# Last stage of a convolution, attention and expert kernel: loop written out, another order on TensorE and VectorE, GpSimd adds eight experts to four

## What is computed

```
t = t + attention(layernorm(t))                        # and attention's own residual
z = layernorm(t)
p = softmax(z @ router_w + router_b)                   # 8 experts
top_p, top_i = top_k(p, 2);  top_p = top_p / sum(top_p)
t = t + sum over the two of top_p * (z @ expert_w[top_i] + expert_b[top_i])
out = t, back as (16, 32, 56, 56)
```

## Time and profile before

| | us |
|---|---|
| median of three runs | 2783.09 |
| profiled execution, its own time | 2785.88 |
| its span in the trace | 2784.1 |
| VectorE busy | 2365.9 (85%) |
| TensorE busy (matmuls) | 2433.0 (87%) |
| ScalarE busy | 1600.0 (57%) |
| GpSimd busy | 406.9 (15%) |
| mean granted TensorE clock | 0.908 |

### The profile page before, as it was taken

One profiled execution on the slowest core, in us unless ns is written; L12 is line 12 of the kernel. 1 busy time (PEld: TensorE's weight loads), 2 busy tenths in 40 slices (PEclk: granted clock), 3 DMA queues, 4 the chain that ended last, 5 costly groups with the idle time before them and its releaser, 6 DMA issues. The chain is left out here.

```text
span 2784.1 us, 48279 instructions
## 1 busy us (share of the span) xinstructions
PE 2433.0 (87%) x18454; PEld 985.0 (35%) x18454; DVE 2365.9 (85%) x4218; ACT 1600.0 (57%) x2106; POOL 406.9 (15%) x456
## 2 busy tenths in 40 slices
PE   3888878379999999999999999999999987777776
PEld 1343333112222222222222222222222246666665
DVE  4567776689999999999999999999999927888886
ACT  1143343247777777777777777777777753233232
POOL 0021121300000000000000000000000004445455
PEclk9989999579999999999999999999999986666666
DMA  7687692510210221201202202202200011223221
GB/s 172 172 222 225 188 271 96 169 33 1 59 40 21 59 94 30 59 22 38 59 10 50 59 1 59 59 1 59 59 1 24 24 53 65 71 74 101 70 70 24
DMA packets 68108, 206.19 MB, mean 74 GB/s; under 512 B 20630, under 2 KB 33554, under 8 KB 61234
## 3 DMA queue, kind: packets, MB, share of 16 engines
q1 hardware_dynamic: 64034, 185.27, 24.0%
q0 software_dynamic: 3040, 15.57, 1.5%
q10 hardware_dynamic: 816, 2.46, 0.3%
HBM read 80.14 MB, written 61.31 MB: 51 GB/s over the span
## 5 line engine op out<-in xcount | busy, mean ns | idle before, releaser
L1333 DVE TENSOR_REDUCE at_XM<-at_psX 128x1 f32<-128x448 f32 x2688 | 1546.2, 619 | 92.2 <-PE at_psX L1184 71.3
L1250 ACT ACTIVATE at_PR<-at_psS 128x896 f32<-128x896 f32 x1344 | 1162.9, 915 | 455.0 <-PE at_psS L1160 452.9
L1202 PE MATMUL at_psV<-at_PR,at_V 128*32 128x448 f32 x5376 | 645.2, 552 | 0.1
L1160 PE MATMUL at_psS<-at_US,at_KS 128*128 128x448 f16 x2688 | 636.2, 356 | 1.7 <-DMA at_US<-at_mrow 1.1
L1184 PE MATMUL at_psX<-at_KS,at_US 64*128 64x448 f16 x1344 | 490.4, 365 | 65.2 <-DVE at_XM L1333 42.8
L1184 PE MATMUL at_psX<-at_KS,at_UH 64*128 64x448 f16 x1344 | 490.4, 365 | 0.0
L1184 PEld LDWEIGHTS at_psX<-at_KS,at_US 64*128 64x128 f16 x1344 | 124.6, 93 | 721.2 <-DVE at_XM L1333 661.5
L1160 PEld LDWEIGHTS at_psS<-at_US,at_KS 128*128 128x128 f16 x2688 | 200.9, 98 | 274.3 <-ACT at_PR L1250 119.3
L1299 POOL CAST at_mrow<-at_mt 7x128 f16<-7x128 f32 x64 | 17.9, 279 | 1613.3 <-DVE at_mt L1352 1260.4
L1602 POOL TENSOR_TENSOR fi_WE<-fi_WE 128x256 f32<-128x256 f32 (+1 forms) x224 | 212.9, 979 | 172.8 <-DVE fi_WE L1656 172.1
L1656 DVE TENSOR_TENSOR fi_WE<-fi_psE,fi_WT 128x512 f32<-128x512 f32 (+1 forms) x208 | 132.7, 666 | 43.9 <-PE fi_psE L1505 33.9
(11 more groups left out here) (205 smaller groups left out, 2101.4 us busy)
## 6 DMA issues: line engine op xcount, KB each, us to landing
sums<-at_O SPq DMA_DIRECT2D x16, 1568.0 KB, 6.3
fi_SUMS<-sums SPq DMA_DIRECT2D x16, 1568.0 KB, 6.6
sb_stacks<-sb_T SPq DMA_DIRECT2D x64, 270.5 KB, 7.2
sb_stacks<-sb_Xp SPq DMA_DIRECT2D x64, 248.8 KB, 8.4
sb_stacks<-sb_Xp SPq DMA_DIRECT2D x64, 248.0 KB, 5.6
sb_stacks<-sb_T SPq DMA_DIRECT2D x64, 172.5 KB, 10.0
at_KS<-key_stacks SPq DMA_DIRECT2D x32, 208.0 KB, 6.8
fi_RES<-residual SPq DMA_DIRECT2D x16, 400.0 KB, 7.0
```

The source lines that it names most:

```text
L1160: last = nc.tensor.matmul(psS[:, at % 2, k, 0:TILE], KS[:, b, (2 * c + k) * P:(2 * c + k + 1) * P], US[:, b, t * TILE:(t + 1) * TILE], sta ...
L1202: last = nc.tensor.matmul(psV[C * q:C * q + C, 0:TILE], V[:, b, G * k + q, :], PR[:, (n * 2 * STEPS + 2 * q4 + q // 2) % PRS, q % 2, :], s ...
L1250: nc.scalar.activation(PR[:, f % PRS], psS[:, at % 2, :, 0:TILE], ACT.Exp).then_inc(p_ready, 1)
L1333: nc.vector.tensor_reduce(o, psX[:, (at + j) % 3, 0:TILE], AX.X, ALU.max).then_inc(x_done, 1)
```

## The change

1. finish is written out for all steps, without the loop; beyond and the register waits go.
2. TensorE's order in a step becomes: project(n + 1) both halves; experts(n - 1, 2 to 6); then six times four or five token transposes and one of the units 7 to 12; the router's first set after unit 10 and the others after unit 12; experts(n, 0 1); sums(n - 1).
3. VectorE's order becomes: weigh 0 and 1 ahead of the sum over channels, weigh 2 ahead of centring, weigh 3 4, sum of squares, weigh 5, root, scale, weigh 6, Z16, weigh 7 to 12, invert both halves and divide the first, top-k, divide the second. The mean is no longer an instruction of its own.
4. The end of the top-k chain multiplies by the reciprocal once instead of twice.
5. newton_rsqrt has three instructions instead of four, in prepare too.
6. GpSimd adds only eight to four, 7 additions an image. TensorE sums the four and T1: five matmuls a set, 70 records an image.

```
 def newton_rsqrt(link, eng, r, v, t):
     link(eng.tensor_tensor(t, r, r, ALU.mult))
-    link(eng.tensor_tensor(t, t, v, ALU.mult))
-    link(eng.tensor_scalar(t, t, -0.5, 1.5, ALU.mult, ALU.add))
-    return link(eng.tensor_tensor(r, r, t, ALU.mult))
+    link(eng.scalar_tensor_tensor(out=t, in0=t, scalar=-0.5, in1=v, op0=ALU.mult, op1=ALU.mult))
+    return link(eng.scalar_tensor_tensor(out=r, in0=t, scalar=1.5, in1=r, op0=ALU.add, op1=ALU.mult))
...
-        def steps(eng, step):
-            for n in range(FIRST):
-                step(n, n % TURN, n // 2)
-            with eng.Fori(0, (N - TURN) // TURN) as i:
-                for n in range(FIRST, FIRST + TURN):
-                    step(i * TURN + n, n % TURN, i * 2 + n // 2)
-            for n in range(N - 1, N + 1):
-                step(n, n % TURN, n // 2)
+        def steps(step):
+            for n in range(N + 1):
+                step(n, n % TURN, n // 2)
...
-                    for e in range(E // 4 + 1):
-                        v = (WE[:, s, e] if e < E // 4 else T1[:, c, G * s:G * s + w // C]).rearrange("p q c -> p (q c)")
+                    for e in range(E // 2 + 1):
+                        v = (WE[:, s, e] if e < E // 2 else T1[:, c, G * s:G * s + w // C]).rearrange("p q c -> p (q c)")
...
                 if more:
-                    project(n + 1, mb, r + b, (0,))
-                if old:
-                    experts(m, mb, (2, 3, 4))
-                if more:
-                    project(n + 1, mb, r + b, (1,))
-                if old:
-                    experts(m, mb, (5, 6))
+                    project(n + 1, mb, r + b)
+                if old:
+                    experts(m, mb, range(2, 7))
                 if new:
                     pe.wait_ge(z16_ready, n + 1)
                     pe.wait_ge(z_high, n * 2 + 2)
-                for s in range(KSETS):
+                for i, u in enumerate(range(7, NU)):
                     if new:
-                        turn_tokens(n, s)
+                        turn_tokens(n, range(NC * i // (NU - 7), NC * (i + 1) // (NU - 7)))
                     if old:
-                        experts(m, mb, (s + 7,))
+                        experts(m, mb, (u,))
+                    if new and u == 10:
+                        router(n, b, 0)
                 if new:
-                    router(n, b)
-                if old:
-                    experts(m, mb, (11, 12))
-                if new:
+                    for k in range(1, KSETS):
+                        router(n, b, k)
                     experts(n, b, (0, 1))
                 if old:
                     sums(m, mc)
...
-                if beyond(n, 0):
-                    for s in range(QSETS + 1):
-                        if s < QSETS:
-                            pool.wait_ge(we_ready, n * NU - NU + min(2 * s + 2, NU))
-                            fold(s, E // 2).then_inc(half_folded, 1)
-                        if s >= 1:
-                            pool.wait_ge(half_folded, n * QSETS - QSETS + s)
-                            fold(s - 1, E // 4).then_inc(folded, 1)
+                if n > 0:
+                    for s in range(QSETS):
+                        pool.wait_ge(we_ready, n * NU - NU + min(2 * s + 2, NU))
+                        fold(s, E // 2).then_inc(folded, 1)
...
-                weigh(m, mb, (0,))
+                weigh(m, mb, (0, 1))
                 dve.wait_ge(t1_ready, n + 1)
                 mark(nc.vector.tensor_reduce(lsum[:], T1[:, c], AX.X, ALU.add))
+                weigh(m, mb, (2,))
                 settled()
-                mark(nc.vector.tensor_scalar(lsum[:], lsum[:], 1.0 / C, None, ALU.mult))
-                weigh(m, mb, (1,))
-                settled()
-                nc.vector.tensor_tensor(XH[:], T1[:, c], per_token(lsum[:]), ALU.subtract).then_inc(t1_cen, 1)
-                weigh(m, mb, (2,))
+                nc.vector.scalar_tensor_tensor(out=XH[:], in0=per_token(lsum[:]), scalar=-1.0 / C, in1=T1[:, c],
+                                               op0=ALU.mult, op1=ALU.add).then_inc(t1_cen, 1)
+                weigh(m, mb, (3, 4))
                 dve.wait_ge(t1_sq, n + 1)
                 link(nc.vector.tensor_reduce(lvar[:], SQ[:], AX.X, ALU.add))
                 nc.vector.tensor_scalar(lvar[:], lvar[:], 1.0 / C, LN_EPS, ALU.mult, ALU.add).then_inc(t1_var, 1)
-                weigh(m, mb, (3, 4))
+                weigh(m, mb, (5,))
...
                 nc.vector.memset(XH[:, :, 0:1], 1.0).then_inc(xh_ready, 1)
+                weigh(m, mb, (6,))
...
-                weigh(m, mb, range(5, NU))
+                weigh(m, mb, range(7, NU))
+                if nxt:
+                    invert(n + 1, 0)
+                    invert(n + 1, 1)
+                    settled()
+                    divide(n + 1, (c + 1) % TURN, 0)
...
+                dve.wait_ge(gap_exp, n + 1)
+                mark(nc.vector.tensor_scalar(g1[:], g2[:], 1.0, None, ALU.add))
                 settled()
+                mark(nc.vector.tensor_tensor(SEL2[:], SEL2[:], per_token(g2[:], E), ALU.mult))
+                mark(nc.vector.reciprocal(g1[:], g1[:]))
                 settled()
+                link(nc.vector.tensor_tensor(SEL1[:], SEL1[:], SEL2[:], ALU.add))
+                mark(nc.vector.tensor_tensor(WT[:, b], SEL1[:], per_token(g1[:], E), ALU.mult))
                 if nxt:
                     divide(n + 1, (c + 1) % TURN, 1)
-                dve.wait_ge(gap_exp, n + 1)
-                link(nc.vector.tensor_scalar(g1[:], g2[:], 1.0, None, ALU.add))
-                link(nc.vector.reciprocal(g1[:], g1[:]))
-                mark(nc.vector.tensor_tensor(g2[:], g2[:], g1[:], ALU.mult))
-                mark(nc.vector.tensor_tensor(SEL1[:], SEL1[:], per_token(g1[:], E), ALU.mult))
                 settled()
-                link(nc.vector.tensor_tensor(SEL2[:], SEL2[:], per_token(g2[:], E), ALU.mult))
-                link(nc.vector.tensor_tensor(WT[:, b], SEL1[:], SEL2[:], ALU.add))
```

More of the change, by code:

```diff
@@ L42 @@
 GR = 2 * XW
-ORDER_0, ORDER = 15, 51
-ORDER_F = 29
+ORDER_0, ORDER = 14, 46
 class Ahead(NamedTuple):
@@ L1456, in step @@
                 b = c % 2
-                if beyond(n, 0) and (not isinstance(n, int) or n + 1 < N):
+                if n > 0 and n + 1 < N:
                     load(n + 1, 1 - b)
-                if beyond(n, 1):
+                if n > 1:
                     store(n - 2, b)
-            steps(sp, step)
+            steps(step)
             store(N - 1, 1)
@@ L1468, in _, with project @@
         def _(pe):
[L1469 to L1473, removed]
-                    if beyond(n, 0):
+            def project(n, b, r):
+                pe.wait_ge(sums_in[b], (r + 1) * 16)
+                for h in range(2):
+                    if n > 0:
                         pe.wait_ge(o_done, n * 2 + h - 1)
@@ L1526, in step @@
                 m, mb, mc = n - 1, 1 - b, (c - 1) % TURN
-                old = beyond(n, 0)
-                new = not isinstance(n, int) or n < N
-                more = not isinstance(n, int) or n + 1 < N
+                old = n > 0
+                new = n < N
+                more = n + 1 < N
                 if more:
-                    project(n + 1, mb, r + b, (0,))
+                    project(n + 1, mb, r + b)
                 if old:
-                    experts(m, mb, (2, 3, 4))
-                if more:
-                    project(n + 1, mb, r + b, (1,))
-                if old:
-                    experts(m, mb, (5, 6))
+                    experts(m, mb, range(2, 7))
                 if new:
@@ L1555, in _ @@
             pe.wait_ge(fin.w_ready, 1)
-            project(0, 0, 0, (0, 1))
-            steps(pe, step)
+            project(0, 0, 0)
+            steps(step)
         @block.scalar
@@ L1570, in step @@
                 b = c % 2
-                if not isinstance(n, int) or n < N:
+                if n < N:
                     act.wait_ge(t1_cen, n + 1)
@@ L1587, in step @@
                         act.wait_ge(k_full, n * KSETS + s + 1)
-                        if s == 0 and beyond(n, 1):
+                        if s == 0 and n > 1:
                             act.wait_ge(e_full, n * NU - NU)
@@ L1594, in step @@
                     nc.scalar.activation(g2[:], gap[:], ACT.Exp).then_inc(gap_exp, 1)
-            steps(act, step)
+            steps(step)
             to_image(N - 1, 1, (N - 1) // 2)
@@ L1629, in _ @@
             done = [0]
-            base = [0]
             def mark(ins):
@@ L1636, in settled @@
             def settled():
-                dve.wait_ge(order, base[0] + done[0])
+                dve.wait_ge(order, done[0])
             def link(ins):
@@ L1652, in weigh @@
                     dve.wait_ge(e_full, n * NU + u + 1)
-                    if u % 2 == 0 and beyond(n, 0):
+                    if u % 2 == 0 and n > 0:
                         dve.wait_ge(set_done, n * QSETS - QSETS + u // 2 + 1)
@@ L1675, in step @@
```

(7 more changed lines are left out.)

81 lines of the change are left out of this document (36 added, 45 removed).

## The result

| | kernel before | changed kernel |
|---|---|---|
| median, us | 2782.77 (2777.23 to 2784.76, 4 runs) | 2801.78 (2799.86 to 2804.66, 4 runs) |
| profiled execution, its span | 2785.88, 2784.1 | 2803.19, 2801.3 |

The ratio is 1.0064 (95% interval 1.0052 to 1.0076): the change costs 19 us. The forecast was 2844, slower by 61. Its sign is right, its size is not. Two executions lie far off all others and are in none of the ratios, one of 2871.66 us of the kernel before and one of 5190.82 us of the kernel before with its loop written out; nothing here shows what made them slow.

The account below looks back on a forecast made before the run. The prediction took VectorE's instruction order to bound the kernel before. Last-stage images +67.3, image 0 -2.7, the end -1.5 and first stage -2 made +61 on 2785.9, 2847; that execution being 2.8 above the median, 2844 (range 2797 to 2880).

Parts of the forecast that it names:

- The step held to be decisive: On TensorE, 50 projection records ahead of experts 2 to 6 take 8.1 us; weighing 2 starts 8.4 late.
- weighing 2 to the first token: VectorE's stretch from weighing 2 to the next image's first token transposition, forecast to go from 8.9 to 9.9 us.
- first token to the sums: TensorE from first token transposition to start of sums, forecast 7.1 us for 7.6, bounds 6.3 and 8.1.
- sums, 70 records: TensorE's sums with 28 more records at 0.118 each, forecast 9.4 us for 6.1, bounds 8.3 to 10.4.
- projection and hand-over: TensorE between sums and weighing 2: projection 8.1 us, expert 2's two matmuls and the hand-over 0.7.
- top-k of 6.4: VectorE's top-k, forecast to fall from 10.1 to 6.4 us through lost stretches, line 1741, inversions and first division.
- the end: After 2764, GpSimd's 12.18 us falls to about 8.5, TensorE partly replacing it: -1.5 us (0 to -4.5).
- rival (1): TensorE's clock holds: sums 8.3, projection 6.0, image 32.0 us, in all 2803 us; chance 0.20.
- The first stage: 20 Newton chains each lose one instruction of 0.2 us, DMA waits hiding about half: -2 us (0 to -4.4).
- The new wait for the residual: VectorE's sum over channels waits for GpSimd's 1.88 us residual, until 2.1 us after weighing 0.
- TensorE's seven sets take its place in part: After 2764, TensorE's seven sets replace only part of GpSimd's saved time, within the forecast of -1.5 us.
- Rival (3): TensorE does not hold VectorE in the last stage: 26.8 us an image, 2732 us in all; chance 0.07.

Follow-up runs that it names:

- the best kernel: Changed kernel with one projection half moved behind expert 3 and the other behind expert 6: 2728.05 us, 0.9793 of the kernel before.
- the experiment on the clock: Changed kernel with one wait added, TensorE starting each step's sums only when VectorE has the top-k chain's gap: 2886.09 us, a single execution.

## Why the prediction was right in its mechanism, and which step of it failed

**The step held to be decisive is the cause.** Both halves of the projection ahead of expert 2 hold weighing 2. Put into the kernel before alone, this costs 15.6 us; put back as it was in the changed kernel, it gives back 15.6, most of the 19. The 74 us of the best kernel are another comparison: a place that neither kernel had, behind expert 3 and behind expert 6, which also frees what the other parts had won and the old place hides.

**The pieces of an image**, images 2 to 14, forecast against measured:

| piece | forecast | measured, mean (range) |
|---|---|---|
| weighing 2 to the first token | 9.9 | 9.97 (9.97 to 9.98) |
| first token to the sums | 7.1 | 6.46 (6.02 to 6.88) |
| sums, 70 records | 9.4 | 8.00 |
| projection and hand-over | 8.8 | 7.62 (6.02 to 8.56) |
| image | 35.2 | 32.06 |

VectorE's piece is exact, and its top-k of 6.4 too (2328.82 to 2335.22 in image 1). All three pieces of TensorE came out short, together 3.2 us an image. With VectorE's 0.07 against it the image is 3.14 short, 40.9 over 13, and the median missed by 42. That the rest is so small is partly luck, since larger misses beside it cancel: the end took 4.8 more than forecast, and the last stage began 5.8 earlier in this execution. The largest term is the sums. I took 70 records at a clock that rises during them, since that is how 11 of the 14 were before. All 14 of the changed kernel ran at the high clock; windows of line 1510 alone (columns us, PE, PEld, clock, DMA), the first two and the sum of the 14:

```profile
2328.71:2336.71 8.00, 8.00 (x70) 7.68 (x70) 1.00 0.01 2
2361.84:2369.84 8.00, 8.00 (x70) 7.69 (x70) 1.00 0.01 2
...
sum 112.00, PE 111.98 PEld 107.55; mean PE 8.00 PEld 7.68
```

Before, TensorE paused twice between the last tokens and the sums, 1.2 to 1.8 us in all (the expectation of the experiment on the clock has 1.0 to 1.3, which is too little). The clock had risen ahead of the sums in 11 of the 14 steps; in 8 of these it fell again around their start, in 3 it held, and in the other 3 steps it rose only during the sums. But the length of the pause alone does not decide: with the same two pauses, 0.32 and 1.01, the clock held in one step and fell in another. TensorE's timeline behind the second pause and a window over the sums, once for each:

```profile
2364.59 0.61 PE L1505 MATMUL fi_psE<-fi_wz,fi_ZS 128*128 128x256 f16 x4 [1.01 <-DVE fi_WE L1656]
2365.10:2369.90 4.80, 4.80 (x43) 4.51 (x42) 4.56 (x11) 0.23 (x1) 2.92 (x5) 1.00 0.00 0
...
2545.84 0.61 PE L1505 MATMUL fi_psE<-fi_wz,fi_ZS 128*128 128x256 f16 x4 [1.01 <-DVE fi_WE L1656]
2546.80:2550.10 3.30, 3.30 (x17) 3.30 (x17) 3.09 (x8) 0.00 (x0) 2.47 (x5) 0.50 0.00 0
```

With experts 7 to 12 among the tokens and the router split, one pause of 0.6 to 0.8 is left, the clock rose ahead of all 14 sums and held, and so it did in all kernels here with that order but the one with the pause added. That the order is what does it fits all of them; which part of it, the shorter pause or the denser work ahead, is not shown. The start came 0.6 earlier on average, the more so the sooner the clock rose: 6.02 us from the first token to the sums where it rose 3.0 us after the first token, 6.88 where it rose after 5.1. Sums and start together are 2.0 of the 3.2.

The second term is the projection. I let the clock fall 2.6 to 3.9 us after the sums, in the middle of the projection; it fell after 3.0 to 6.0 in these 13 images. Windows of line 1465 alone, three images:

```profile
2466.71:2474.80 8.09, 8.09 (x50) 7.95 (x50) 0.69 0.01 3
2500.11:2507.53 7.42, 7.42 (x50) 7.28 (x50) 0.76 0.00 0
2532.01:2537.77 5.76, 5.76 (x50) 5.65 (x50) 1.00 0.01 3
```

The first is the 8.1 of my sum, the last is rival (1)'s 6.0, and the mean lies between. The fall itself, in the second of them:

```profile
2501.10:2504.00 2.90, 2.90 (x28) 2.90 (x27) 0.58 (x1) 0.00 (x0) 0.78 (x1) 0.99 0.00 0
2504.00:2505.00 1.00, 1.00 (x7) 1.00 (x6) 0.00 (x0) 0.00 (x0) 0.00 (x0) 0.50 0.00 0
```

TensorE is busy without a gap on both sides of it (by the modelled ends of the trace), as before. By the Trainium skill, "TensorE: Matmul & The Clock Gate", section on why this matters for your kernels, TensorE kept busy holds the high clock; for the sums that is what happened, for the projection it is not.

So **rival (1)**, at 32.0 an image and 2803, came nearest in time, but its mechanism holds for the sums only, and in 10 of 13 images not for the whole projection. That it meets the time is luck: its projection of 6.0 is too short, and its start of 7.1 and sums of 8.3 too long by about as much. The failed step is the price of the sums and of the projection, both taken at the old kernel's clock although the change itself alters what TensorE does ahead of them: 9.4 us for the sums, which took 8.00, and 8.8 for the projection with its hand-over, which took 7.62.

**Smaller steps.** The first stage was forecast at -2; the mean over all kernels is -2.3, but their spread of 4 us either way neither shows nor excludes it. Line 81 takes over the stretch, 1.13 us in the median, as I had it. The new wait for the residual is there, 0.79 to 0.80 ahead of the sum over channels. Image 0 gained 1.6 of the 2.7 forecast (22.92 for 24.50), since that wait of 0.8 comes there too; I had left it out. Image 1 took 29.4 (29.6), and the stretch from the first token of image 14 to that of image 15 took 25.7 (27.1), short by the same pieces, start and sums.

**The end went the other way.** I had -1.5 for the last 20 us, since GpSimd does less there. From the first weighing of the last step to the end it takes 23.4 us for 20.0. GpSimd is indeed done sooner, but nobody waits for it. Expert 2 stands behind sums(14), so VectorE waits 1.02; and TensorE's last sums, with 28 more records, start at the low clock. Windows near the beginning and the end of these sums:

```profile
2786.00:2789.00 3.00, 3.00 (x15) 3.00 (x16) 0.99 (x2) 0.00 (x0) 2.29 (x3) 0.50 0.02 5
...
2793.00:2796.40 3.40, 3.38 (x30) 2.99 (x28) 0.00 (x0) 0.00 (x0) 0.00 (x0) 1.00 0.00 0
```

They take 10.3 us, where 42 records had taken 7.9, also from the low clock on. In the best kernel the same 70 records ran at the high clock and took 8.1, behind the same gaps of 0.2 between the experts; why the clock held there is not shown. The step that failed is "TensorE's seven sets take its place in part": they take its place and more.

**Rival (3)**, VectorE alone at 26.8 an image and 2732, did not happen here, but the best kernel comes to it: 25.4 to 26.3 an image, 2728. What it needed was not a faster TensorE but nothing long ahead of expert 2.

**Parts alone, on the kernel before:** Newton -8.7, loop written out -13.6, adding to four -8.8, both halves of the projection together +15.6. VectorE's and TensorE's other new orders were not tried alone. The sum of the parts does not give the whole: one TensorE call, in the wrong place, hides what VectorE gained.

## What to carry to other kernels

When an engine that bounds the loop is made faster, write down for the other engine what it does between the last product that the first one has and the next one that it needs, and keep long work whose result is due late out of that gap. Put such work where its consumer still has other input, and in pieces. Price matmuls at the clock that the new order will leave them, not at the clock of the old trace.

## What the runs showed of the hardware that was not expected

- The projection's matmuls (float32, 33 columns) do not hold the high clock though they leave no gap by the trace's modelled ends: it falls 3.0 to 6.0 us after the sums, and 50 records then take 5.76 to 8.10 us by where it falls, 9.68 when they start later.
- With pauses of 1.3 to 1.8 us in all ahead of the sums, TensorE lost the high clock in 8 steps of the kernel before, and with 1.3 it kept it in 3; with one of 0.6 to 0.8 in the changed kernel it lost it in none of 14.
- Writing out the loop gave 13.6 us, twice the two jumps of 3.36. The loop's other images became some 0.6 shorter; that the waits made from a register cost this is argued from the images in and out of the loop, not shown by a run of its own.
- The place at which the last stage starts varies by 4 us either way (2285.0 to 2292.6 in eight profiles, one of each of eight kernels whose first two stages are the same), so a single pair of profiles says nothing of a few us there.
